# A cross-attention kernel: x is split earlier, wq_lo moves to GpSimd, and three groups of weights are loaded behind the packing of keys and queries

## The reference

```python
q = _split_heads(hidden_states @ Wq.T, H)          # x: (2, 2048, 640), H = 20 heads of D = 32
k = _split_heads(text @ Wk.T, H)                   # text: (2, 77, 1024)
v = _split_heads(text @ Wv.T, H)
scores = jnp.einsum('bhsd,bhld->bhsl', q, k) * sm_scale
probs = jax.nn.softmax(scores, axis=-1)
out_text = _merge_heads(jnp.einsum('bhsl,bhld->bhsd', probs, v))
out = out_text @ Wo.T + bo                         # the ip part has no tokens
return out + residual                              # residual = x
```

## Time and profile before

| | |
|---|---|
| median of three runs | 444.87 us |
| profiled execution | 445.5 us |
| its span | 443.7 us |
| busy: TensorE, VectorE, ScalarE, GpSimd | 432.1, 314.3, 250.7, 228.2 us |
| granted clock of TensorE | 0.995 of full |

### The profile page before, as it was taken

The page is one execution under the profiler, slowest core; times in us unless marked ns, Lnnn a source line. Parts: engine busy times, 40 slices in busy tenths (PEclk is TensorE's granted clock), DMA queues, the critical chain, the costliest instruction groups (busy, mean ns, idle before and its releaser), DMA issues.

```text
span 443.7 us, 8269 instructions
## 1 busy us (share of the span) xinstructions
PE 432.1 (97%) x2538; PEld 313.7 (71%) x2538; DVE 314.3 (71%) x509; ACT 250.7 (57%) x509; POOL 228.2 (51%) x184
## 2 busy tenths in 40 slices
PE   8989989899999999999999999999999999999996
PEld 6967665576777767776777766777777766777675
DVE  0465896877869586967869586967869586966663
ACT  1728876846565464756565464756565464755510
POOL 7403796836546373636546373636546373634440
PEclk9999989999999999999999999999999999999999
DMA  8995433535344534445344534455345443445203
GB/s 286 398 394 161 160 101 127 192 123 189 121 143 164 178 136 145 173 180 195 120 144 160 178 139 144 169 182 194 123 143 166 154 157 120 148 154 177 73 24 120
DMA packets 39615, 72.70 MB, mean 164 GB/s; under 512 B 5024, under 2 KB 6176, under 8 KB 39584
## 3 DMA queue, kind: packets, MB, share of 16 engines
q1 hardware_dynamic: 28784, 52.62, 33.2%
q10 hardware_dynamic: 10800, 19.67, 13.9%
HBM read 28.81 MB, written 10.49 MB: 89 GB/s over the span
## 4 chain that ended last, share of the span: by engine, by line
PE 91%; DVE 3%; ACT 2%; issue 1%; DMA 1%; POOL 1%; DVEq 0%; ACTq 0%; POOLq 0%
PE ps_q L676 30%; PE ps_o L676 26%; PE ps_s L722 9%; PE ps_pv L729 6%; PE ps_m L708 6%; PE ps_den L734 4%; PE ps_m L773 1%; DMA q_packed<-mxT 1%; PE ps_s L647 1%; PE ps_m L713 1%; PE ps_o L660 1%; PE ps_q L773 1%; ACT p_f L415 1%; PE ps_q L639 1%; DVE x_f L573 1%
## 5 line engine op out<-in xcount | busy, mean ns | idle before, releaser
L325 POOL TENSOR_TENSOR p_lo<-p_f,p_hi 77x512 f16<-77x512 f32 x120 | 147.7, 1236 | 169.6 <-ACT p_hi L419 169.6
L415 ACT ACTIVATE p_f<-ps_s 77x512 f32<-77x512 f32 x160 | 95.0, 593 | 47.4 <-PE ps_s L722 47.4
L419 ACT ACTIVATE p_hi<-ps_s 77x512 f16<-77x512 f32 x160 | 93.9, 587 | 1.0 <-PE ps_den L734 0.8
L534 DVE TENSOR_REDUCE mx<-ps_m 128x4 f32<-128x308 f32 x160 | 68.8, 471 | 18.0 <-PE ps_m L708 17.5
L676 PE MATMUL ps_q<-x_hi,wq_hi 128*128 128x512 f32 x200 | 79.9, 399 | 0.0
L676 PE MATMUL ps_q<-x_hi,wq_lo 128*128 128x512 f32 x200 | 78.5, 393 | 0.0
L676 PE MATMUL ps_q<-x_lo,wq_hi 128*128 128x512 f32 x200 | 78.5, 392 | 0.0
L527 DVE TENSOR_TENSOR q_lo<-ps_q,q_hi 128x512 fp32r<-128x512 f32 x40 | 27.6, 690 | 68.7 <-ACT q_hi L398 68.7
L398 ACT CAST q_hi<-ps_q 128x512 fp32r<-128x512 f32 x40 | 23.4, 585 | 91.8 <-PE ps_q L676 91.8
L676 PE MATMUL ps_o<-attn_hi,wo_hi 128*128 128x512 f32 x170 | 69.5, 409 | 0.0
L676 PE MATMUL ps_o<-attn_lo,wo_hi 128*128 128x512 f32 x170 | 66.9, 394 | 0.0
(11 more groups left out here) (105 smaller groups left out, 602.5 us busy)
## 6 DMA issues: line engine op xcount, KB each, us to landing
q_packed<-q_hi SPq DMA_DIRECT2D x80, 256.0 KB, 2.5
x_f<-in_x SPq DMA_DIRECT2D x40, 256.0 KB, 3.1
q_packed<-q_lo SPq DMA_DIRECT2D x40, 256.0 KB, 3.2
x_res<-in_x ACTq DMA_DIRECT2D x35, 256.0 KB, 2.8
out<-out_sb ACTq DMA_DIRECT2D x35, 256.0 KB, 2.6
wk_sb<-in_wk SPq DMA_DIRECT2D x8, 320.0 KB, 5.2
wv_sb<-in_wv SPq DMA_DIRECT2D x5, 512.0 KB, 10.9
wq_sb<-in_wq SPq DMA_DIRECT2D x5, 320.0 KB, 9.0
```

The source lines that it names most:

```text
L325: nc.gpsimd.tensor_tensor(p_lo[:, i, :], p_f[:, i, :], p_hi[:, i, :], ALU.subtract).then_inc(plo_pool, 1)
L415: nc.scalar.activation(p_f[:, i, :], ps_s[i % 2][0:L, :], ACT.Exp, scale=SCALE).then_inc(pf_done, 1)
L419: nc.scalar.activation(p_hi[:, i, :], ps_s[i % 2][0:L, :], ACT.Exp, scale=SCALE).then_inc(phi_done, 1)
L534: nc.vector.tensor_reduce(mx[:, g % RS, :, tt], ps_m[tt % 2][:, 0:HG * L].rearrange("p (h k) -> p h k", k=L), AX_X, ALU.max).then_inc(max_ ...
```

## The change

Three things move. First, x: VectorE's chunks become 0 and 2, GpSimd's 1, 3 and 4. In every block step (b,2) now ends with x_hi of chunks 0 and 1 of the next block on ScalarE, x_lo of chunk 0 on VectorE and x_lo of chunk 1 on GpSimd; step (b,3) does the rest, also for block 1. Second, VectorE: `wq_low` of groups 1 to 4 goes to GpSimd, the copies `wq_hi` are made one step earlier by ScalarE, and in the fill `scale_v` stands behind the first two maxima. Third, the loads: only groups 0 and 1 of wq and wv are asked for in the setup; group 2 is asked for behind the packing of the keys, 3 behind the packing of the queries of (0,0), and 4 behind that of (0,1).

```diff
--- before.py
+++ after.py
@@ -95,12 +95,16 @@
     def is_last(t):
         return isinstance(t, int) and t == NB - 1
 
+    def has_next(t):
+        return not isinstance(t, int) or 0 <= t < NB - 1
+
+    def x_first_at(t, g):
+
+        return t + 1 if g == 2 and has_next(t) else None
+
     def x_split_at(t, g):
 
-
-        if g != 3 or (isinstance(t, int) and not 1 <= t < NB - 1):
-            return None
-        return t + 1
+        return t + 1 if g == 3 and has_next(t) else None
 
     def attn_split_at(t, g):
 
@@ -135,6 +139,7 @@
 
 
     DVE_CHUNKS, POOL_CHUNKS = (1, 3), (0, 2, 4)
+    X_DVE_CHUNKS, X_POOL_CHUNKS = (0, 2), (1, 3, 4)
     DVE_HEADS, POOL_HEADS = (0,), (1, 2, 3)
 
@@ -256,12 +261,16 @@
                 if c % 2 == 0:
                     sp.dma_start(ctx_sb[:, c:c + 2, :], ctx[:, c:c + 2, :]).then_inc(ctx_in[c // 2], 16)
                 sp.dma_start(wk_sb[:, c, :], wk[:, c, :]).then_inc(wk_in[c], 16)
-            for g in range(G):
+
+            def load_w(g):
                 sp.dma_start(wq_sb[:, g, :], wq[:, g, :]).then_inc(wq_in[g], 16)
                 if g == 0:
                     load_x(0, range(G))
                     sp.dma_start(bias[:, :], bo).then_inc(bias_in, 16)
                 sp.dma_start(wv_sb[:, g, :], wv[:, g, :]).then_inc(wv_in[g], 16)
+
+            load_w(0)
+            load_w(1)
             sp.wait_ge(const_done, 1)
             sp.wait_ge(q_cleared, RS)
             for terms, src, done in (((0, 1), k_hi, khi_done), ((2,), k_lo, klo_done)):
@@ -269,6 +278,7 @@
                 for term in terms:
                     sp.dma_start(k_packed[term_rows(term), :, :, :].bitcast(F32),
                                  src[:, :, :].bitcast(F32)).then_inc(kpack_in, 16)
+            load_w(2)
 
 
             def load_max(t, g):
@@ -295,6 +305,8 @@
                     sp.dma_start(wo_sb[:, c, :], wo[:, c, :]).then_inc(wo_in[c], 16)
                 if exists(shift(t, g, 2)[0]):
                     pack_q(*shift(t, g, 2))
+                if isinstance(t, int) and nth(t, g) in (-2, -1):
+                    load_w(nth(t, g) + G)
             run(sp, step, *LOOP)
 
         @block.gpsimd
@@ -331,7 +343,13 @@
                     nc.gpsimd.tensor_tensor(attn_lo[:, c, :], attn[:, c, :], attn_hi[:, c, :].bitcast(F32),
                                             ALU.subtract).then_inc(alo_pool, 1)
 
-            x_low(0, POOL_CHUNKS)
+            x_low(0, X_POOL_CHUNKS)
+
+            def wq_low(c):
+                pool.wait_ge(wq_hi_done, c + 1)
+                pool.wait_ge(wq_lo_done, c)
+                nc.gpsimd.tensor_tensor(wq_lo[:, c, :], wq_sb[:, c, :], wq_hi[:, c, :].bitcast(F32),
+                                        ALU.subtract).then_inc(wq_lo_done, 1)
 
             def wo_low(c):
                 pool.wait_ge(wo_hi_done, c + 1)
@@ -341,19 +359,21 @@
             def step(t, g):
                 xt, (at, chunks) = x_split_at(t, g), attn_split_at(t, g)
                 mine = [c for c in POOL_CHUNKS if c in chunks]
+                for c in query_group(t, g):
+                    wq_low(c)
                 if xt is not None:
-                    x_low(xt, POOL_CHUNKS[:2])
+                    x_low(xt, X_POOL_CHUNKS[1:2])
                 if exists(t):
                     p_low(t, g, 1)
                 if xt is not None:
-                    x_low(xt, POOL_CHUNKS[2:])
+                    x_low(xt, X_POOL_CHUNKS[2:])
                 attn_low(at, mine[:1])
                 if exists(t):
                     p_low(t, g, 2)
                     p_low(t, g, 3)
                 attn_low(at, mine[1:])
-                if isinstance(t, int) and (t, g) == (0, 2):
-                    x_low(1, POOL_CHUNKS)
+                if x_first_at(t, g) is not None:
+                    x_low(x_first_at(t, g), X_POOL_CHUNKS[:1])
                 for c in wo_chunks(*shift(t, g, -1)):
                     wo_low(c)
 
@@ -443,11 +463,12 @@
             x_high(0, range(G))
             start_k()
             diagonal_k(0, range(HG))
+            w_high(wq_in, wq_sb, wq_hi, wq_hi_done, (1,))
 
             def step(t, g):
                 xt, (at, chunks) = x_split_at(t, g), attn_split_at(t, g)
                 if xt is not None:
-                    x_high(xt, range(0, 3))
+                    x_high(xt, (2,))
                 if exists(t):
                     exponentials(t, g, 0)
                     exponentials(t, g, 1)
@@ -468,11 +489,11 @@
                 for tile in out_tiles(*shift(t, g, 1)):
                     load_residual(*tile)
                 attn_high(at, [c for c in (4,) if c in chunks])
+                if x_first_at(t, g) is not None:
+                    x_high(x_first_at(t, g), (0, 1))
                 if exists(shift(t, g, 2)[0]):
                     q_high(*shift(t, g, 2))
-                if isinstance(t, int) and (t, g) == (0, 2):
-                    x_high(1, range(G))
-                w_high(wq_in, wq_sb, wq_hi, wq_hi_done, query_group(t, g))
+                w_high(wq_in, wq_sb, wq_hi, wq_hi_done, query_group(*shift(t, g, 1)))
                 if isinstance(t, int) and t == 0 and g <= 1:
                     diagonal_k(1, range(HG // 2 * g, HG // 2 * (g + 1)))
                 w_high(wo_in, wo_sb, wo_hi, wo_hi_done, wo_chunks(*shift(t, g, -1)))
@@ -585,7 +606,7 @@
             nc.vector.tensor_reduce(head_mask[:, :], ident[:, :].rearrange("p (d i) -> p i d", i=HG),
                                     AX_X, ALU.max).then_inc(mask_done, 1)
             wq_low((0,))
-            x_low(0, DVE_CHUNKS)
+            x_low(0, X_DVE_CHUNKS)
             start_k()
             dve.wait_ge(bias_in, 16)
 
@@ -594,20 +615,18 @@
                 last_t, last_g = shift(t, g, -1)
                 if isinstance(t, int) and t == NB:
                     attn_low(at, 3)
-                if xt is not None:
-                    x_low(xt, DVE_CHUNKS[:1])
-                for v in value_group(t, g):
-                    scale_v(v)
                 if exists(shift(t, g, 1)[0]):
                     reduce_max(*shift(t, g, 1), 0)
                     reduce_max(*shift(t, g, 1), 1)
+                for v in value_group(t, g):
+                    scale_v(v)
                 if exists(t):
                     p_low(t, g, 0)
                 if exists(shift(t, g, 1)[0]):
                     reduce_max(*shift(t, g, 1), 2)
                     reduce_max(*shift(t, g, 1), 3)
                 if xt is not None:
-                    x_low(xt, DVE_CHUNKS[1:])
+                    x_low(xt, X_DVE_CHUNKS[1:])
                 for v in value_group(t, g):
                     v_low(v)
                 if exists(last_t):
@@ -617,13 +636,12 @@
                     finish_out(*tile)
                 if 1 in chunks:
                     attn_low(at, 1)
+                if x_first_at(t, g) is not None:
+                    x_low(x_first_at(t, g), X_DVE_CHUNKS[:1])
                 if exists(shift(t, g, 2)[0]):
                     q_low(*shift(t, g, 2))
                 if 1 in chunks and 3 in chunks:
                     attn_low(at, 3)
-                wq_low(query_group(t, g))
-                if isinstance(t, int) and (t, g) == (0, 2):
-                    x_low(1, DVE_CHUNKS)
 
             run(dve, step, *LOOP)
             for k in range(G):
@@ -677,13 +695,13 @@
-            def wait_chunk(hi, lo_dve, lo_pool, t, c):
+            def wait_chunk(hi, lo_dve, lo_pool, dve_chunks, pool_chunks, t, c):
 
                 pe.wait_ge(hi, G * t + c + 1)
-                if c in DVE_CHUNKS:
-                    pe.wait_ge(lo_dve, len(DVE_CHUNKS) * t + DVE_CHUNKS.index(c) + 1)
+                if c in dve_chunks:
+                    pe.wait_ge(lo_dve, len(dve_chunks) * t + dve_chunks.index(c) + 1)
                 else:
...
```

More of the change, by code:

```diff
@@ L678, in project @@
                     last.then_inc(done, 1)
-            def wait_chunk(hi, lo_dve, lo_pool, t, c):
+            def wait_chunk(hi, lo_dve, lo_pool, dve_chunks, pool_chunks, t, c):
                 pe.wait_ge(hi, G * t + c + 1)
-                if c in DVE_CHUNKS:
-                    pe.wait_ge(lo_dve, len(DVE_CHUNKS) * t + DVE_CHUNKS.index(c) + 1)
+                if c in dve_chunks:
+                    pe.wait_ge(lo_dve, len(dve_chunks) * t + dve_chunks.index(c) + 1)
                 else:
-                    pe.wait_ge(lo_pool, len(POOL_CHUNKS) * t + POOL_CHUNKS.index(c) + 1)
+                    pe.wait_ge(lo_pool, len(pool_chunks) * t + pool_chunks.index(c) + 1)
             def project_q(t, g, chunks):
@@ L693, in ready @@
                     if g == 0:
-                        wait_chunk(xhi_done, xlo_dve, xlo_pool, t, c)
+                        wait_chunk(xhi_done, xlo_dve, xlo_pool, X_DVE_CHUNKS, X_POOL_CHUNKS, t, c)
                 if 0 in chunks and exists(shift(t, g, -1)[0]):
@@ L751, in ready @@
                     if k == 0:
-                        wait_chunk(ahi_done, alo_dve, alo_pool, t, c)
```

(3 more changed lines are left out.)

## The result

The changed kernel takes 442.53 us (median of 4 runs, 442.35 to 442.67), the kernel before in the same job 444.92 (4 runs, 443.78 to 445.57): ratio 0.9939, 95% interval 0.9916 to 0.9961. That is 2.4 us less; 2.8 were forecast.

The account below looks back on a forecast made before the run. TensorE, busy 432.1 of 443.7 us, was taken as the bound. The terms -1.41 - 0.55 + 0.45 - 1.25 = -2.76 us gave 442.7 from the profiled execution, 442.1 from the median; 8-in-10 range 439.4 to 444.3.

Parts of the forecast that it names:

- Loads behind the packed keys: Fill, before the first scores: maxima land at about 30.4 instead of 32.5, so TensorE's whole wait goes, -1.41 us.
- wq_lo to GpSimd: Fill step (0,2): GpSimd's wo_lo ends earlier and stands less in the way of VectorE's p_lo, -0.55 us.
- The loop: Steps (b,3) lose 0.51 us, a 0.3 us wait for GpSimd's p_lo arises at (b,4): -1.25 us over six blocks.
- The fill of x: Step (0,3): about 2.3 us wait for GpSimd's x_lo at the last chunk, slower clock behind it: +0.45 us.
- clock term: Step (0,3): the old slow stretch costs 1.55 us; a new fall after the change was taken as 1.0 us.
- B: Rival: GpSimd in time in the loop, clock up in (0,3); -5.8 us, with half of the doubts 439.3; chance 0.20.
- D: Rival: VectorE delays GpSimd's five operations, which then bound (b,3) and (b,4); 452.3, or 445.5 to 448; chance 0.06.
- C: Rival: loop waits 0.6 us or more (443.4), or late weights block ScalarE in the fill, costing 1.5 us (443.6); chance 0.21.
- the signs that were named for "right": Maxima before 31.2; (0,2) wait mostly gone; (b,3) 9.8; six p_lo waits, 0.2 to 0.45; (0,3) 2 us wait, slow clock.

Follow-up runs that it names:

- experiment 1: The kernel before with only the new order of the loads, groups 2 to 4 of wq and wv behind the packing: 444.29 us, ratio 0.9986.
- experiment 10: The changed kernel with only wq 2 asked for in the setup, ahead of the key packing: 442.81 us, ratio 0.9941.
- experiment 5: Kernel of experiment 4 with wq 2 asked for ahead of the keys, and loads, copies and subtractions of groups 3 and 4 one step later: 440.59 us.
- experiment 7: The edits of experiment 5 and experiment 6 together: 438.70 us, ratio 0.9861.
- experiment 9: Kernel of experiment 7 with wq 4 asked for one step earlier, its copy and subtraction back where the changed kernel has them: 437.67 us, ratio 0.9859.
- experiment 2: The kernel before with only wq_lo on GpSimd, wq_hi one step earlier and the v scales behind the first two maxima: 444.02 us, ratio 0.9981.
- experiment 4: The changed kernel with x_hi of chunk 3 ahead of the exponentials on ScalarE in (b,3): 439.62 us, ratio 0.9898.
- experiment 8: The changed kernel with the v scales back in front of the first two maxima: 442.82 us, ratio 0.9953.
- experiment 6: Kernel of experiment 4 with VectorE's x_lo of chunk 2 ahead of its p_lo and second pair of maxima: 438.85 us, ratio 0.9869.

## Why the prediction was right, and where it was not

**Loads behind the packed keys: direction right, size too large.** Predicted -1.41, measured -0.72 in the profiled execution and 0.7 to 1.2 less over the five traces with this order (experiment 1). The step that failed is the landing of the maxima: 30.4 was forecast, by taking 2.15 us off the old landing, as if all that stayed ahead of them drained as before; they landed at 31.79. It isn't the price of the 0.85 MB taken away, which at 342 GB/s would be more, 2.5 us. The chain of waits after shows both things that were missed:

```profile
20.58 5.72 DMA wq_sb<-in_wq
26.30 0.02 issue
26.32 0.73 ACT wq_hi L407
...
27.49 4.30 DMA q_packed<-mxT
```

wq 2 landed at 26.30, not at 24.8, so the slack of 0.5 was gone; v_hi, which follows it, started at 26.95 instead of 26.01. Yet that cost the maxima only 0.39 us (27.49 against 27.10); in experiment 10, without ScalarE's wait, they are asked for at 27.24 and take 5.01, with no gain. The larger part is the queue: the maxima took 4.30 us from their issue, where the prediction has 3.3 (27.10 to 30.4). Experiment 1 shows it without ScalarE's wait (26.98, then 4.59), and experiments 5, 7 and 9 show what would have met the forecast: with groups 3 and 4 behind the maxima the wait is 0. Why the queue moves less at 22 to 24 us, where it is busy, is not shown.

**wq_lo to GpSimd: right.** -0.55 against -0.62, by the p_lo that was named; experiment 2 has it alone.

**The loop: right in mechanism and size.** GpSimd's x_lo was to start 4.3 us into (3,3); it did at 4.32. Its last p_lo was to end at 10.65; it ended at 10.67. TensorE was to start at 10.8; it did at 10.81:

```profile
213.40 0.40 PE L747 MATMUL ps_pv<-p_hi,v_hi 77*32 77x512 f16 x4
...
214.41 0.40 PE L747 MATMUL ps_pv<-p_lo,v_hi 77*32 77x512 f16 x4 [0.18 <-POOL p_lo L337]
```

The page's way of counting gives this wait as 0.18 us, since the ends of matmuls are modelled. The distance between the two rows is 1.01 instead of 0.66, a loss of 0.35. And 6 x 0.3 of waiting is 1.8, where the step starts give 1.92. GpSimd's loss to one VectorE neighbour was 1.61 - 1.16 = 0.45 us, by 0.03 the row's 0.42. That is less than the 0.6 to 0.8 by which the loop would have gained nothing, though near the 0.55 that VectorE still needs when GpSimd has ended (below). Experiment 4 shows that the chain was the right one: only its head moved, and the whole loss in (b,4) went.

**The fill of x: wrong in its parts.** I had one wait of 2 us for GpSimd at the last chunk and a clock that falls. There were four short waits, 2.12 us in all, three of them for VectorE, and the clock stayed up, so +0.45 came out as -0.20. But that is one execution. In experiment 10, whose program is the same in this stretch, and in 8, where only the v scales stand elsewhere, there is a wait of 1.41 us for GpSimd's x_lo at the last chunk, with 0.20 before it: the kind that was forecast, at 1.6 instead of 2.3 us. Two things make the difference. The first is VectorE's x_lo of chunk 0, which stood still behind two GpSimd operations in a row; first VectorE's row, then GpSimd's:

```profile
56.55 3.19 DVE L543 TENSOR_TENSOR x_lo<-x_f,x_hi 128x512 fp32r<-128x512 f32 x1
59.66 0.68 DVE L548 TENSOR_TENSOR q_lo<-ps_q,q_hi 128x512 fp32r<-128x512 f32 x1
...
56.39 1.28 POOL L328 TENSOR_TENSOR x_lo<-x_f,x_hi 128x512 fp32r<-128x512 f32 x1
57.63 1.56 POOL L356 TENSOR_TENSOR wo_lo<-wo_sb,wo_hi 128x640 fp32r<-128x640 f32 x1
```

It delayed q_lo, TensorE's first wait. In experiments 4, 8 and 10 the same subtraction, 0.15 or 0.16 us behind the same GpSimd operation, took 1.67 to 1.69 us, and wo_lo had to wait for it (2.00 to 2.02).

The second is the clock. Experiments 1 and 2 split x as the kernel before does; with the clock up they take 9.05 and 9.06 us for (0,3), where the profiled execution before took 9.83. So its slow stretch was worth 0.78, half of the 1.55 that I put into the old step. Against these, (0,3) and (0,4) cost 17.00 - 16.42 = +0.6, and in experiments 8 and 10 +0.2 (16.59 and 16.60). The forecast without either clock term is 11.65 - (12.16 - 1.55) = +1.0, so the waits of the new order were put too high. The sign in the ledger is the clock's, not the change's.

**Rivals.** B (GpSimd in time in the loop, the clock up in (0,3)) failed on the six waits; the clock did stay up. D failed since only one of GpSimd's five operations was lengthened. C's blocked ScalarE occurred, 4.45 us for wq 2, but gave back 0.39 us instead of 1.5. Three of the signs that were named for "right" did not come in the profiled execution: the maxima landed behind 31.2, and in (0,3) there was neither a wait of 2 us for GpSimd nor a fall of the clock.

## What to carry to other kernels

When loads are reordered, don't take the old rate for what stays in front: only a run shows how the new mix drains. And ask what still stands ahead of the small DMA that everyone waits for. Two placements found by reading which engine's queue held the head of the chain (x_hi of chunk 3 on ScalarE, x_lo of chunk 2 on VectorE) were together worth at least as much as the change itself: 3.7 us by the medians and 3.1 by the ratios (experiment 6 against the changed kernel), where the change is 2.4 and 2.7. Gains in the fill don't add by themselves, since work that is moved off one step's front lands at the next one's (experiments 5 and 7), and that has to be placed too (experiment 9).
